# Two packed attentions: VectorE copies the turned maxima one maximum earlier, and in the last stage takes unit 0's heads ahead of the splitting of the maxima

## The reference, cut to what matters

```python
# second block, for each sequence; x is [128 channels, 256]
q, k, v = Wq @ x + bq, Wk @ kv + bk, Wv @ kv + bv          # 16 heads of 8 channels
attn = softmax(einsum('bhqd,bhdk->bhqk', q / sqrt(8), k))
mean = einsum('bhqk,bhkd->bhqd', attn, v)
ex2  = einsum('bhqk,bhkd->bhqd', attn, v * v)
std  = sqrt(relu(ex2 - mean * mean))
out  = instance_norm(x) * std + mean
...
# fourth block; q and kv are the layer-normed rows with position codes
attn = softmax(einsum('bhqd,bhkd->bhqk', q @ Wq, kv @ Wk) / sqrt(8))
y    = merge_heads(einsum('bhqk,bhkd->bhqd', attn, kv @ Wv)) @ Wo
r    = y + q
out  = r + gelu(layer_norm(r) @ W1 + b1) @ W2 + b2
```

## Time and profile before

| | us |
|---|---|
| median of 3 runs | 2410.79 |
| lowest and highest | 2407.82, 2411.61 |
| the profiled execution, whole | 2414.69 |
| its span, first to last instruction | 2412.6 |
| the two packed stages in it | 283 and 275 |

### The profile page before, as it was taken

How to read it: one execution, slowest core, us unless ns; L and a number is a source line. 1 busy time by engine, 2 the same in 40 slices (tenths; PEclk the granted TensorE clock), 3 DMA queues, 4 the chain that set the end, 5 groups by cost and what they waited for, 6 DMA issues and landing times. The chain is left out here.

```text
span 2412.6 us, 52415 instructions
## 1 busy us (share of the span) xinstructions
PE 2202.7 (91%) x17289; PEld 1777.0 (74%) x17289; DVE 1792.9 (74%) x4688; ACT 1445.6 (60%) x4012; POOL 710.1 (29%) x995
## 2 busy tenths in 40 slices
PE   5999999998999999996989999689999979799998
PEld 4898989997899989996976666456666569566654
DVE  6666666677666666666759889698888765789885
ACT  3554545555555555555747777577777756477874
POOL 2111111112211111103025554466666510334300
PEclk8999999999999999998979999899999989699999
DMA  5001111010000110002000000100000000000001
GB/s 127 23 23 24 23 24 58 23 23 1 23 23 23 23 24 23 1 1 70 0 8 13 8 11 4 36 8 1 9 17 17 7 5 0 13 10 11 7 4 36
DMA packets 72952, 47.25 MB, mean 20 GB/s; under 512 B 29232, under 2 KB 71600, under 8 KB 72752
## 3 DMA queue, kind: packets, MB, share of 16 engines
q1 hardware_dynamic: 72752, 44.62, 7.1%
HBM read 41.45 MB, written 2.10 MB: 18 GB/s over the span
## 5 line engine op out<-in xcount | busy, mean ns | idle before, releaser
L1908 DVE TENSOR_REDUCE maxima<-bank 128x2 f32<-128x512 f32 x512 | 331.1, 683 | 35.9 <-PE bank L1005 34.2
L1547 ACT ACTIVATE probs_t<-bank 128x512 f32<-128x512 f32 x512 | 282.5, 601 | 69.8 <-PE bank L996 67.7
L1421 ACT ACTIVATE wide_probs_t<-bank 128x256 f32<-128x256 f32 x256 | 98.4, 384 | 303.2 <-PE bank L881 301.0
L1426 ACT ACTIVATE wide_probs<-bank,wide_neg_max 128x129 f32<-128x129 f32 x512 | 184.1, 365 | 116.2 <-DVE wide_neg_max L1759 112.4
L2262 POOL TENSOR_TENSOR wide_columns<-wide_pair_columns,zero 128x8 f32<-128x8 f32 x16 | 3.3, 207 | 741.6 <-DVE x L1791 697.8
L1433 ACT ACTIVATE wide_heads_high<-bank,wide_columns 128x128 fp32r<-128x128 f32 x512 | 160.3, 365 | 85.2 <-PE bank L895 83.6
L1764 DVE RECIPROCAL wide_inverse<-wide_sums 128x2 f32<-128x2 f32 x256 | 42.5, 166 | 226.2 <-ACT wide_probs L1426 226.2
L1766 DVE TENSOR_SCALAR wide_probs<-wide_probs,wide_inverse 128x128 f32<-128x128 f32 x512 | 178.7, 391 | 9.0
L1778 DVE SCALAR_TENSOR_TENSOR wide_heads_low<-bank,wide_columns,wide_heads_high 128x128 fp32r<-128x128 f32 x512 | 155.1, 345 | 35.6 <-ACT wide_heads_high L1433 30.8
L996 PE MATMUL bank<-q_packed,k_packed 32*128 32x256 f32 x1024 | 172.3, 339 | 8.2 <-ACT probs_t L1547 7.4
L1005 PE MATMUL bank<-k_packed,q_packed 32*128 32x256 f32 x1024 | 175.0, 344 | 3.9 <-ACT q_packed L1532 2.2
(11 more groups left out here) (302 smaller groups left out, 6846.8 us busy)
## 6 DMA issues: line engine op xcount, KB each, us to landing
cn<-in_ctx SPq DMA_DIRECT2D x48, 128.0 KB, 2.0
wide_pair_weights<-in_L_xattn_wq SPq DMA_DIRECT2D x16, 256.0 KB, 2.9
wide_pair_weights<-in_L_xattn_wk SPq DMA_DIRECT2D x16, 256.0 KB, 3.2
wide_pair_weights<-in_L_xattn_wv SPq DMA_DIRECT2D x16, 256.0 KB, 3.5
wide_pair_weights<-in_L_xattn_wo SPq DMA_DIRECT2D x16, 256.0 KB, 3.4
q_packed<-max_rows SPq DMA_DIRECT2D x256, 4.0 KB
wide_ctx_rows<-in_ctx SPq DMA_DIRECT2D x4, 512.0 KB, 7.2
x<-in_x SPq DMA_DIRECT2D x4, 512.0 KB, 8.2
```

The source lines that it names most:

```text
L1426: last = act.activation(probs0[:, b, h, :], wide_scores[b % 2][:, h * KEYS0:(h + 1) * KEYS0], ACT.Exp, bias=neg_max0[:, b, h:h + 1], accum ...
L1547: act.activation(probs_t[j % 8][:, :], shifted_bank[j % 2][:, :], ACT.Exp, bias=0.0).then_inc(s.exp_ready, 1)
L1908: dve.tensor_reduce(maxima[pack // 2][:, b, pack % 2, :], head_scores[packed_scores(1 - u, j)][:, :].rearrange("p (a k) -> p a k", a=UNITS ...
```

## The change

VectorE's list alone is altered, in two places of its window. In both packed stages `copy_maxima(n + 1, 0)` at step 9 now stands ahead of that step's maximum instead of behind it. In the last stage (`third`) `split_maxima(n + 1, 0)` at step 8 now stands behind `release`, so behind the reciprocal and the product of unit 0's heads, instead of ahead of them. The number of instructions stays the same, and the lists of the other engines don't change.

```diff
-                    if following and j == TURN_MAXIMA[0] - 1:
+                    if following and j == TURN_MAXIMA[0] - 1 and not third:
                         split_maxima(n + 1, 0)
...
                     release(n, at, u, j)
+                    if following and j == TURN_MAXIMA[0] - 1 and third:
+                        split_maxima(n + 1, 0)
+                    if following and j == TURN_MAXIMA[0]:
+                        copy_maxima(n + 1, 0)
...
                     if core and j == TURN_MAXIMA[1]:
                         copy_maxima(n, 1)
-                    if following and j == TURN_MAXIMA[0]:
-                        copy_maxima(n + 1, 0)
                     own(n, at, u, j)
```

## The result

| | kernel before | changed kernel |
|---|---|---|
| median of the comparison, us | 2410.49 | 2396.43 |
| lowest and highest of 4 runs | 2407.82, 2411.61 | 2391.77, 2399.77 |
| the profiled execution, whole (span) | 2414.69 (2412.6) | 2399.77 (2398.1) |

The ratio is 0.9949, with a 95% interval of 0.9928 to 0.997, which is 12.3 us; by the medians it is 14.1 us, by the two spans 14.5. In a later comparison the changed kernel had 2397.59 against 2409.18, ratio 0.9954 (0.9938 to 0.9969), so 11.6 us by the medians. The medians in this document leave out four executions of 3566 to 5876 us (one of the kernel before, one each of e2, e6 and e11).

What follows compares the result with a forecast made beforehand. VectorE and TensorE were taken to lead in turn in the packed stages. Last stage 6.5 plus first stage 6.7 made 13.2 us; from the median 2410.79 that gave 2397.6, say 2397.5 us, range 2393 to 2405.5.

Steps and rivals of the forecast that it cites:

- falls gone, last stage near 0.5 a window: Both packed stages: first stage's clock falls end, last stage gains about 0.50 us a window; chance 45%.
- First stage at full clock: nothing: First packed stage, windows without a fall: TensorE's wait moves from the sums to L983, some 0.7 us; gain nil.
- The falls: 6.2 us, taken as gone: First packed stage: five falls of the clock to 0.50, together 6.2 us, end with the wait for the copy.
- the case of the clock: First packed stage, rival: the falls stay or move, stage gains 3.0 us, time 2401.3; chance 27%.
- The last stage: 6.5: Last packed stage: ten windows 5.0, four last ones 1.4, first window 0.1; bounds 3.8 and 8.4 us.
- the maximum of step 8 starts at 2207.29 as before: Last stage, VectorE: heads and splitting change places, heads start 0.44 us earlier, the following maximum's start is unchanged.
- The copy doesn't wait: Last stage, VectorE: maxima are turned 0.2 us before the moved copy, which starts 0.60 us earlier without waiting.
- VectorE's wait for the values gone, the placed queries earlier: Last stage: VectorE's 0.30 us wait for TensorE's values goes; placed queries start at 2210.96 instead of 2211.46.
- Nothing changes elsewhere: Rest of the program: same instructions in the same order, so only the two packed stages, 283 and 275 us, can change.
- The sums are held by ScalarE: Both stages, rival: ScalarE holds step 11's sums, the copy's 0.6 us is worth nothing, 2408 to 2411; chance 8%.
- New falls at L983: First stage, rival: the longer wait ahead of L983 brings ten more falls, +14 us, time 2415; chance 5%.
- VectorE-bound: Last stage, rival: VectorE becomes the bound, gain only 3.8 us there, time 2404.0; chance 15% (with half the gain).

Runs made afterwards that it cites:

- e2: Changed kernel with both copies back in their old places, only the last stage's heads ahead of the splitting; 2405.75 us, ratio 0.9979 to the kernel before.
- e6: Kernel before, but TensorE issues three of four groups of step 11's sums ahead of the wait for the copy, both stages; 2406.47 us, ratio 0.9988.
- e11: Kernel before with the copy moved up in the first packed stage alone, a repeated run; 2406.04 us, ratio 0.9985.
- e5: Changed kernel, but in the first stage TensorE's sums of step 11 also wait for the maximum of step 9; 2400.84 us, ratio 0.9962.
- e8: Changed kernel with the splitting behind unit 0's heads in the first stage too, run on the second chip; 2390.83 us, ratio 0.9928 to the kernel before.
- e1: Changed kernel with the last stage's splitting back ahead of the heads, so only the copy is moved, both stages; 2404.63 us, ratio 0.9976.
- e7: The changed kernel itself, unaltered, run again on a second chip; 2397.59 us.
- e4: Changed kernel with the splitting behind unit 0's heads in the first stage too; 2395.3 us, ratio 0.9939 to the kernel before.

## Why the prediction was right, point by point

The forecast was 2397.5, the median 2396.4: right in direction and size, and its main case, "falls gone, last stage near 0.5 a window", is what happened. That the time was met to about 1 us is partly luck. By the means of the traces the last stage gave 7.8 us instead of 6.5 and the first stage 5.0 instead of 6.7, and the parts that were taken as unchanged added up to only 0.6. The second comparison gives 11.6 us instead of the first one's 14.1.

- **First stage at full clock: nothing.** Right. Windows without a fall took 16.55, 16.52 and 16.43 us before and 16.55, 16.52 and 16.41 after, and the wait ahead of L983 went to 0.70, as the text had it.
- **The falls: 6.2 us, taken as gone.** Right, and shown from both sides by e5 and e6. The ten windows took 163.9 us instead of 171.0, a little under the assumed 164.8. The first window's 0.5 was 0.15. Together 7.3 against 6.7, for this trace (the table's 7.1 begins behind that first window and has the last one, 0.1 us longer, in it); by the average of three traces 5.0. The prediction read one execution's number of falls as the kernel's; the case of the clock should have been spread from 0 to 6.2 on that account too.
- **The last stage: 6.5, measured 7.9.** The direction of each step was right, the size of the window's gain was not. The ten windows with a wait at L1078 gave 6.4 instead of 5.0, or 0.64 each; the four late ones 1.8 instead of 1.4; the first -0.4 instead of +0.1. That last one is the clock's: the first window ran at half clock for 17 us in the changed kernel and for 15 in the kernel before. In e5 and e8, which have the same order in the last stage and 15 us at half clock, it takes 18.98 and 19.05 us against 19.13, about the 0.1 expected.
- **The step that failed: "the maximum of step 8 starts at 2207.29 as before".** The working took the splitting and the heads as two pairs that change places and keep their lengths, so that the heads start at 2206.35 and the maximum at 2207.29. They don't. The kernel before, VectorE, ahead of the earlier trace rows:

```profile
2205.56 0.68 DVE L1908 TENSOR_REDUCE maxima<-bank 128x2 f32<-128x512 f32 x1
2206.35 0.22 DVE L1873 CAST max_parts<-maxima 128x16 fp32r<-128x16 f32 x1
```

  The splitting reads that very maximum, and the code has it wait for it: it starts 0.79 us behind the maximum's start. In the changed kernel the reciprocal, which reads other data, follows the same maximum after 0.60, and when the splitting comes, that maximum is done. From maximum to maximum VectorE needs 1.45 us (2199.38 to 2200.83) instead of 1.73 (2205.56 to 2207.29). e2 shows 1.45 as well, and e1, with the old order, 1.59 to 1.69. The window of the earlier trace rows is one of the longer kind: every second one of the kernel before has about 1.63, and the ten windows saved 0.23 us each on average. So VectorE's list, which the prediction took as the bound of the window at a gain of 0.50, was itself 0.2 to 0.3 shorter. And the heads come 0.63 us earlier instead of 0.44 (0.60 instead of 1.23 behind the maximum), which is close to the 0.64 that a window gained. It also explains the one sign of the prediction that missed: L1078's idle time went to under 0.1 us in eight of the ten windows, where 0.25 had been expected. The row that tells it was at hand: its start is in the trace, though not among.
- **"The copy doesn't wait."** Right, the first window aside. There it waits 0.55 us for L976, at half clock; behind it the moved copy has no wait of more than 0.03 us in any window of the last stage. The sign of being wrong that was named, a copy held by L976, is what e1 shows (0.35 in ten windows), not the changed kernel.
- **VectorE's wait for the values gone, the placed queries earlier.** Right; no wait of VectorE for L1097 is left, and the chain shows TensorE leading.
- **Nothing changes elsewhere.** True of the code, not of the time. Over three traces of before and two of the changed kernel the mean span fell by 13.4 us: 2.6 ahead of the first stage's second window, 5.0 in the first stage, -4.4 between, 7.8 in the last, 2.4 in the tail (rounding apart). The last stage is the part that repeats best: 260.6 us in all three traces of before, 252.7 and 252.8 in the two of the changed kernel.
- **The rivals.** "The sums are held by ScalarE" falls with e2 and e6, whose sums move with the copy or without waiting. "New falls at L983" didn't come, with waits of up to 0.70 in 14 windows. "VectorE-bound" was the right question with the wrong number.

## What to carry to other kernels

When two groups of instructions change places on an engine, look at which of them reads what the instruction just ahead wrote: put the one that doesn't behind it, and count the difference in starts (here 0.79 against 0.60 us), since it shortens the engine's own list (by 0.23 us a window here, on average). Two edits that each remove one of two obstacles on a path must be costed together (3.0 and 1.6 alone, 7.9 together). When a row of waits is counted, look which instructions it holds: two copies of a window share a line here, and only one of them was moved. And a fall of the clock seen in one profiled execution is one draw: take two or three traces before its cost goes into a sum.

## What the runs showed of the hardware

- Falls of the granted clock to 0.50 came at a wait of only 0.3 to 0.4 us on a TensorE that was busy for 96% of the stretch (211.58 of 220 us), but waits of up to 0.70 ahead of L983, in 14 windows, brought none (the changed kernel, 1260 to 1495 us). Nor did 0.69 ahead of L1078 with 0.26 ahead of the sums in the last stage of the kernel before. What stands around a wait mattered here, not its length alone; the runs don't show which part of the surroundings it is.

```profile
PE bank L983 <- DVE hidden L1962: 9.3, 14, 0.7
```

- A filled wait of the same length (e6, 1.40 us for sums that take 1.07) brought no fall between 1280 and 1500 us.
- The stretch between the two stages, whose code is the same in all these kernels, took 577.2 to 579.2 us in most traces and 583.1 to 583.2 in three (changed, e7, e6). The clock differs in it: the windows view of it, of the kernel before and then of the changed kernel, has 0.94 and 0.92.

```profile
1507.00:2082.00 575.00, 487.40 (x3892) 354.89 (x3892) 443.14 (x1079) 376.75 (x969) 277.50 (x263) 0.94 0.04 11
```

```profile
1507.00:2082.00 575.00, 490.98 (x3838) 358.48 (x3837) 441.54 (x1078) 371.45 (x958) 274.46 (x260) 0.92 0.04 11
```

  Both traces of the changed kernel are of the longer kind and all three of before of the shorter, while e4 and e5, which differ from the changed kernel in the first stage alone (its order, one more wait), took 578.6 and 578.5. Whether that is tied to the change or to the moment at which the stretch begins is open.
- The Trainium skill (VectorE: DVE Perf Modes, "The DRAIN you can't avoid") has a case where semaphores between VectorE's instructions cost nothing extra. Here the cast of the splitting, which waits for the reduction just ahead, starts 0.79 us after that reduction's start, and the cast of L1880 and the reciprocal, which don't, 0.59 (1383.25 to 1383.84) and 0.60; for these the measurement decides.
